# Attention over four heads at once, with the softmax sums on GpSimd and one VectorE reduce per two heads

## The reference, cut to what matters

```python
qkv = x @ w_qkv                                    # one sequence of 2048 rows, 16 heads of 32
q, k, v = jnp.split(qkv, 3, axis=-1)
q, k, v = (to_heads(q), to_heads(k), to_heads(v))
q = _rope(q, cos, sin)
k = _rope(k, cos, sin)
scores = jnp.einsum('bhqd,bhkd->bhqk', q, k) / jnp.sqrt(jnp.float32(HD))
scores = jnp.where(causal, scores, -jnp.inf)
attn = jax.nn.softmax(scores, axis=-1)
y = jnp.einsum('bhqk,bhkd->bhqd', attn, v)
```

## Time and profile before

| | |
|---|---|
| median of 3 runs | 2595.11 us (2592.67 to 2601.68) |
| the profiled execution's own time | 2602.47 us |
| its span, first to last instruction | 2600.7 us |
| attention stage, from its first DMA to the read of its result | 1050.4 to 1774.4 us |
| whole span: PE, DVE, ACT, POOL busy | 84%, 59%, 42%, 8% |

### The profile page before, as it was taken

The page is one execution under the profiler, slowest core; times in us unless marked ns, Lnnn a source line. Parts: engine busy times, 40 slices in busy tenths (PEclk is TensorE's granted clock), DMA queues, the critical chain, the costliest instruction groups (busy, mean ns, idle before and its releaser), DMA issues. The chain is left out here.

```text
span 2600.7 us, 43768 instructions
## 1 busy us (share of the span) xinstructions
PE 2190.7 (84%) x18800; PEld 1252.6 (48%) x18800; DVE 1537.1 (59%) x2400; ACT 1085.5 (42%) x1046; POOL 199.2 (8%) x225
## 2 busy tenths in 40 slices
PE   6799999999966997699999999993861399999990
PEld 3444444444433442344444444441360388888880
DVE  7768888888848099665665665541345244434423
ACT  5668888888814111044444444441110123223210
POOL 0000000000010043000000000001402200000005
PEclk9899999999988999599999999996955599999995
DMA  7311111121160223402220222006201523323307
GB/s 249 124 40 69 69 47 57 68 69 49 40 251 20 81 113 121 122 8 56 58 51 10 56 58 56 5 9 140 65 17 57 210 105 108 135 106 110 110 25 266
DMA packets 81360, 221.63 MB, mean 85 GB/s; under 512 B 10384, under 2 KB 11536, under 8 KB 72816
## 3 DMA queue, kind: packets, MB, share of 16 engines
q1 hardware_dynamic: 70080, 176.76, 21.2%
q0 software_dynamic: 11088, 42.08, 4.5%
HBM read 154.98 MB, written 59.51 MB: 82 GB/s over the span
## 5 line engine op out<-in xcount | busy, mean ns | idle before, releaser
L449 ACT ACTIVATE m_step<-m_ub,gat_bias 128x2048 bf16<-128x2048 f32 x256 | 494.0, 1992 | 120.6 <-DVE m_mask L526 109.5
L1057 DVE TENSOR_REDUCE t_rm<-t_m 128x1 f32<-128x512 f32 (+3 forms) x640 | 373.5, 608 | 238.7 <-PE t_m L1106 184.2
L1015 ACT ACTIVATE t_E<-t_s 128x1024 f32<-128x1024 f32 (+1 forms) x320 | 292.0, 938 | 424.2 <-PE t_s L1122 222.8
L526 DVE TENSOR_TENSOR m_mask<-m_step,gat_adjT 128x2048 bf16<-128x2048 bf16 x256 | 306.7, 1222 | 84.0 <-ACT m_step L449 72.1
L1106 PE MATMUL t_m<-t_K,t_Q 96*128 96x512 f32 (+3 forms) x640 | 262.3, 445 | 58.1 <-POOL t_trik L994 32.6
L1143 PE MATMUL t_o<-t_E,t_v 128*32 128x512 f32 (+1 forms) x1280 | 282.0, 560 | 0.0
L1143 PE MATMUL t_o<-t_E,t_ones 128*32 128x512 f32 (+1 forms) x1280 | 282.0, 560 | 0.0
L1106 PEld LDWEIGHTS t_m<-t_K,t_Q 96*128 96x128 f32 x640 | 117.3, 197 | 212.4 <-issue 89.5
L566 PE MATMUL m_bd<-m_mask,m_S 128*32 128x512 bf16 x3072 | 211.9, 380 | 8.0 <-DVE m_mask L526 7.7
L1122 PE MATMUL t_s<-t_Q,t_K 97*128 97x512 f32 (+1 forms) x640 | 216.2, 413 | 0.0
L566 PE MATMUL m_bd<-gat_adjT,m_S 128*32 128x512 bf16 x3072 | 211.5, 380 | 4.8 <-PE m_dn L566 4.8
(11 more groups left out here) (278 smaller groups left out, 3126.3 us busy)
## 6 DMA issues: line engine op xcount, KB each, us to landing
a_adj<-in_adj SPq DMA_DIRECT2D x16, 1024.0 KB, 4.9
m_ub<-scratch_uac SPq DMA_DIRECT2D x16, 1024.0 KB, 4.7
e_w1r<-in_L_ffn_w SPq DMA_DIRECT2D x8, 2048.0 KB, 8.0
e_w2r<-in_L_ffn_w SPq DMA_DIRECT2D x8, 2048.0 KB, 8.6
t_Q<-scratch_parts SPq DMA_DIRECT2D x42, 256.0 KB, 6.1
t_K<-scratch_parts SPq DMA_DIRECT2D x42, 256.0 KB, 8.2
scratch_xe<-o_zeros POOLq DMA_DIRECT2D x10, 1024.0 KB, 19.1
e_xe<-scratch_xe SPq DMA_DIRECT2D x8, 1280.0 KB, 9.1
```

The source lines that it names most:

```text
L449: act.activation(step[n % RELUS][:, :], ub[h % 2][:, :], ACT.Relu, bias=bias[:, j, h:h + 1], scale=BIG).then_inc(step_ready, 1)
L526: dve.tensor_tensor(mask[n % MASKS][:, :], step[n % RELUS][:, :], adjT[:, j, :], ALU.min).then_inc(mask_ready, 1)
L1015: act.activation(E[s % 2][hh][:, :, 0:w], ps_s[hh][:, :].rearrange("p (b n) -> p b n", b=2)[:, :, 0:w], ACT.Exp, scale=SCALE).then_inc(exp ...
L1057: dve.tensor_reduce(rm[:, hh, t, ch:ch + 1], ps_m[i % 2][:, 0:w], AX, ALU.max).then_inc(entry_read, 1)
```

## The change

Four heads (a quad) are worked on at once: four quads, 40 steps of one key tile each (160 in all), with queries cut at the diagonal to `BANK - off`. Scores of heads 0, 1 (z = 0) and 2, 3 (z = 1) lie in the four banks of `ps_s`; one exponential covers two heads. `E` has three buffers. TensorE's matmuls with ones no longer read `E`: GpSimd adds the exponentials of two steps into `total`, and `denominators` multiplies that by ones once in two steps, into a bank of its own (`ps_d`), which ScalarE copies out. `values` has four matmuls with the values of four heads, read from `V` (the copy into `v` goes). A piece of the maxima is made for two heads, in the two banks of the single `ps_m`, and one reduce reads both. A piece waits for the one right before it (`entry_read`, n, with nothing given in advance). A quad has 80 such pieces and 4 turns. 14 entries run ahead; the first quad has 70 more in its first 21 steps (`own_until`), and each quad makes 42 of the next one's in its last 19 (`next_until`). Q has one buffer, reloaded chunk by chunk. The rows of ones in K are set by GpSimd, and stores are issued apart for results and denominators.

```diff
-    for c in range(NC):
-        STEPS += [(c, kt, 0, BANK) for kt in range(0, 4 * c, 2)]
-        STEPS += [(c, 4 * c, 0, BANK), (c, 4 * c + 2, 2 * P, 2 * P)]
+    QUADS, G = H // 4, 4
+
+
+    STEPS = [(c, kt, max(0, kt - 4 * c) * P) for c in range(NC) for kt in range(4 * c + 4)]
     NS = len(STEPS)
...
     def pieces(c):
-        return [(hh, t, ch, BANK if ch < t // 4 else (t % 4 + 1) * P)
-                for hh in range(2) for t in range(4 * c, 4 * c + 4) for ch in range(c + 1)]
...
-            at += n + more
-    assert at == ahead, (at, ahead)
+    FIRST_OF = {c: min(i for i, (kind, p) in enumerate(ENTRIES) if kind == "piece" and p[1] // 4 == c) for c in range(NC)}
+
+
+    HALF = NS // 2
+    def even(s, s0, s1, n0, n1):
+        return n0 + (n1 - n0) * (s + 1 - s0) // (s1 - s0)
+
+    AHEAD = 8 + 1 + 16 + 1 + 16
+    def own_until(q, s):
+        if q == 0:
+            if s < 2:
+                return even(s, 0, 2, START, 25)
+            if s < 9:
+                return even(s, 2, 9, 25, 50)
+            return even(min(s, HALF), 9, HALF + 1, 50, NE)
+        return even(min(s, HALF), 0, HALF + 1, AHEAD, NE)
+
+    def next_until(q, s):
+        if q == QUADS - 1 or s <= HALF:
+            return 0
+        return even(s, HALF + 1, NS, 0, AHEAD)
+    START = 14
+
+
+    SUMS = [0]
+    for k in range(QUADS * NS // 2):
+        SUMS.append(SUMS[k] + (2 if STEPS[2 * k % NS][2] < STEPS[(2 * k + 1) % NS][2] else 1))
...
+        Q = st.sb("Q", [P, G, N], F32R)
+        K = [st.sb(f"K{r}", [P, G, N], F32R) for r in range(2)]
+        E = [st.sb(f"E{i}", [P, G, BANK]) for i in range(3)]
+        total = st.sb("total", [P, G, BANK])
...
-        ps_s = [st.ps(f"s{hh}", [P, 2 * BANK]) for hh in range(2)]
-        ps_o = [st.ps(f"o{i}", [P, BANK]) for i in range(2)]
-        ps_m = [st.ps(f"m{i}", [P, BANK]) for i in range(2)]
...
+        ps_s = st.ps("s", [P, G, BANK])
+        ps_o, ps_d = st.ps("o", [P, BANK]), st.ps("d", [P, BANK])
+        ps_m = st.ps("pm", [P, 2, BANK])
...
+                load_k(1)
+                for q in range(QUADS):
+                    more = q + 1 < QUADS
+                    if more:
+                        load_q(q + 1, 0)
+                    store(q, 0)
...
-                for j in range(H // 4):
-                    for r in range(2):
-                        pool.wait_ge(v_free[r], j + 1)
-                        col = (j * 4 + 2 * r) * DH
-                        pool.tensor_copy(v[r][:, :, :, :].rearrange("p t h d -> p t (h d)"),
-                                         V[:, :, ds(col, 2 * DH)]).then_inc(v_in[r], 1)
+                    pool.memset(K[r][ROWS:K1, :, :].bitcast(F32), 1.0).then_inc(k_ones[r], 1)
+                    pool.wait_ge(k_ones[r], 1)
+                for k in range(QUADS * NS // 2):
+                    a = 2 * k
+                    wide, off = STEPS[a % NS][2], STEPS[(a + 1) % NS][2]
+                    if k >= 1:
+                        pool.wait_ge(den_done, k)
+                    for z in range(2):
+                        pool.wait_ge(exp_done[z], a + 2)
+                        two = slice(2 * z, 2 * z + 2)
+                        if wide < off:
+                            pool.tensor_copy(total[:, two, wide:off], E[a % 3][:, two, wide:off]).then_inc(summed[z], 1)
+                        pool.tensor_tensor(total[:, two, off:BANK], E[a % 3][:, two, off:BANK],
+                                           E[(a + 1) % 3][:, two, off:BANK], ALU.add).then_inc(summed[z], 1)
...
+                if u >= 2:
+                    act.wait_ge(d_sent[u % 2], 64 * (u // 2))
+                act.activation(den[u % 2][:, :], ps_d[:, :], ACT.Copy).then_inc(d_copied, 1)
...
+                    for z in range(2):
+                        act.wait_ge(s_full[z], n + 1)
+                        if n >= 3:
+                            act.wait_ge(pv_done, n - 2)
+                            act.wait_ge(summed[z], SUMS[(n - 3) // 2 + 1])
+                        two = slice(2 * z, 2 * z + 2)
+                        act.activation(E[n % 3][:, two, off:BANK], ps_s[:, two, off:BANK], ACT.Exp,
+                                       scale=SCALE).then_inc(exp_done[z], 1)
+
+                    if n >= 3 and (n - 3) % NS in END.values():
+                        u = (n - 3) // NS * NC + STEPS[(n - 3) % NS][0]
+                        denominators_out(act, u)
+                denominators_out(act, QUADS * NC - 1)
...
-                    dve.tensor_reduce(rm[:, hh, t, ch:ch + 1], ps_m[i % 2][:, 0:w], AX, ALU.max).then_inc(entry_read, 1)
+                    h, t, ch, w = what
+                    dve.tensor_reduce(rm[:, h:h + 2, t, ch], ps_m[:, :, 0:w], AX, ALU.max).then_inc(entry_read, 1)
...
+                        pe.wait_ge(m_ready, q * NC + what + 1)
+                        if n >= 1:
+                            pe.wait_ge(entry_read, n)
...
+                    h, t, ch, w = what
...
+                    if n >= 1:
+                        pe.wait_ge(entry_read, n)
+                    diag = ch == c
+                    for z in range(2):
+                        mm = pe.matmul(ps_m[:, z, 0:w], Q[0:ROWS, h + z, t * P:(t + 1) * P],
+                                       K[q % 2][0:ROWS, h + z, ch * BANK:ch * BANK + w], start=True, stop=not diag)
                     if diag:
-                        mm = pe.matmul(ps_m[i % 2][:, w - P:w], ident_b[:, :], triq[:, :], start=False, stop=True)
+                        for z in range(2):
+                            mm = pe.matmul(ps_m[:, z, w - P:w], ident_b[:, :], triq[:, :], start=False, stop=True)
                     mm.then_inc(entry_full, 1)
...
+                    if n >= 1:
+                        pe.wait_ge(exp_done[z], n)
...
+                    for h in (2 * z, 2 * z + 1):
+                        mm = pe.matmul(ps_s[:, h, off:BANK], K[q % 2][0:K1, h, kt * P:(kt + 1) * P],
+                                       Q[0:K1, h, c * BANK + off:(c + 1) * BANK], start=True, stop=not diag)
...
+                    mm.then_inc(s_full[z], 1)
...
+                def values(n):
+                    q, s = divmod(n, NS)
+                    c, kt, off = STEPS[s]
+                    if kt == 0 and n:
+                        pe.wait_ge(o_copied, q * NC + c)
+                    for z in range(2):
+                        pe.wait_ge(exp_done[z], n + 1)
+                    for h in range(G):
+                        mm = pe.matmul(ps_o[h * DH:(h + 1) * DH, off:BANK], V[:, kt, (q * G + h) * DH:(q * G + h + 1) * DH],
+                                       E[n % 3][:, h, off:BANK], start=(kt == 0), stop=(kt == 4 * c + 3))
+                    mm.then_inc(pv_done, 1)
+
+                def denominators(k):
+                    q, s = divmod(2 * k, NS)
+                    c, kt, off = STEPS[s]
+                    last = kt == 4 * c + 2
+                    if kt == 0 and k:
+                        pe.wait_ge(d_copied, q * NC + c)
+                    for z in range(2):
+                        pe.wait_ge(summed[z], SUMS[k + 1])
+                    for h in range(G):
+                        mm = pe.matmul(ps_d[h * DH:(h + 1) * DH, off:BANK], ones[:, :], total[:, h, off:BANK],
+                                       start=(kt == 0), stop=last)
+                    mm.then_inc(den_done, 1)
+
+                pe.wait_ge(setup, 5)
+                own, coming = START, 0
+                for i in range(START):
+                    entry(0, i)
+                for z in range(2):
+                    scores(0, z)
+                for q in range(QUADS):
...
+                        n = q * NS + s
+                        upto, later = own_until(q, s), next_until(q, s)
+                        done = 0
+                        whole = upto - own + later - coming
...
+                            goal = ((whole + 1) // 2, (whole + 1) // 2, whole)[g]
+                            while own < upto and done < goal:
+                                entry(q, own)
                                 own += 1
...
+                                done += 1
+                            while coming < later and done < goal:
+                                entry(q + 1, coming)
+                                coming += 1
+                                done += 1
+                            if g < 2 and n + 1 < QUADS * NS:
+                                scores(n + 1, g)
+                        if n >= 2 and n % 2 == 0:
+                            denominators(n // 2 - 1)
+                        values(n)
+                    own, coming = coming, 0
+                denominators(QUADS * NS // 2 - 1)
```

More of the change, by code:

```diff
@@ L856, in pieces @@
     def pieces(c):
-        return [(hh, t, ch, BANK if ch < t // 4 else (t % 4 + 1) * P)
-                for hh in range(2) for t in range(4 * c, 4 * c + 4) for ch in range(c + 1)]
+        return [(h, t, ch, BANK if ch < t // 4 else (t % 4 + 1) * P)
```

(70 more changed lines are left out.)

309 lines of the change are left out of this document (90 added, 219 removed).

## The result

| | before | after |
|---|---|---|
| median of 4 runs | 2594.38 us (2592.67 to 2601.68) | 2668.69 us (2663.10 to 2673.70) |
| the profiled execution's own time | 2602.47 us | 2664.31 us |
| its span | 2600.7 us | 2662.1 us |
| first scores, last copy | 1094.0, 1770.2 us | 1087.0, 1831.1 us |
| read of the stage's result | 1774.4 us | 1837.4 us |

The change makes the kernel slower: ratio 1.028, 95% interval 1.0247 to 1.0313. Between the profiled executions the read of the stage's result moves by 63.0 us and the whole time by 61.8, so all of it is in this stage.

A forecast was written before the change was run, and what follows sets the result against it. TensorE's program order was taken to bound the kernel before; after, waits at the hand-over of pieces spend the saving. 2602.5 + 7 + 50 = 2659.5 us profiled, less 7.4 for the median: 2652 us, range 2598 to 2706.

The forecast's parts named there:

- The hand-over of a piece: Each two-head piece waits for the reduce of the one before: 2.04 us round trip, 2.51 with values and denominators.
- What leaves TensorE: TensorE's matmuls in the stage: 80 groups of values or ones fewer, 69 us; scores lose 7 us.
- The quads: Times of the stage's four quads: near 250, 170, 170 and 140 us.
- The clock: TensorE's clock in the stage: first 21 steps largely at 1.2 GHz, 38 us; later falls 12; together +50.
- ten falls: Drops of TensorE's clock behind the first 21 steps: ten at 1.2 us each, 12 us.
- Sums and the ends: GpSimd's adds of 1024 columns take 2.4 us; main part starts 5 us sooner; +3 us behind the last copy.
- the ring: Last 19 steps: two sums in the single `total`, then denominators, then the next sums, 6.1 us for two steps.
- GpSimd beside VectorE: VectorE's scaling of maxima could wait for a GpSimd sum, 16 times, up to 38 us; none was put in.
- the last one: Step from profiled execution to median: 7.4 us taken off 2659.5, giving 2652 us.
- the main part: Stage from first scores to last copy: 685 us expected at 2.4 GHz, 9 more than the 676 before.

The follow-up runs named there:

- The filling: The changed kernel with throwaway zero-weight matmuls between neighbouring pieces of the first quad and between the 14 entries ahead: 2644.75 us, ratio 1.0184.
- the kernel with the sums by heads: The changed kernel, but the one buffer of GpSimd's sums is handed over to and from TensorE by two heads: 2664.47 us, ratio 1.0258.

## Why the prediction was right

It said 2652 us (2598 to 2706), slower; the median is 2669. By its steps:

- **The hand-over of a piece.** Expected 2.04 us, with a reduce of 1.23; measured 2.05 and 1.226. With denominators 2.51 expected, 2.40 to 2.52 measured. The experiments confirm that this is the mechanism: a shorter reduce or a second buffer each give over 100 us.
- **What leaves TensorE.** The 69 us can't be read off one row. From the first piece to the last copy TensorE is busy for 684 of 713 us before and for 648 of 774 in after, and the 648 hold the stretches at half speed. The kernel with one-head pieces shows that some 42 us of them can be had.
- **The quads.** Expected 250, 170, 170 and 140; measured from the first scores and the copies:

```profile
1086.98 0.63 PE L1155 MATMUL t_s<-t_Q,t_K 97*128 97x512 f32 x1
...
1350.22 0.68 DVE L1065 COPY t_out<-t_o 128x512 f32<-128x512 f32 x1
...
1519.24 0.68 DVE L1065 COPY t_out<-t_o 128x512 f32<-128x512 f32 x1
...
1691.41 0.68 DVE L1065 COPY t_out<-t_o 128x512 f32<-128x512 f32 x1
...
1831.09 0.69 DVE L1065 COPY t_out<-t_o 128x512 f32<-128x512 f32 x1 [44.20 <-PE t_o L1169]
```

  263.2, 169.0, 172.2 and 139.7, in sum 744 us for the 735 of my sum (685, and 50 for the clock). The last three come to 480.9 us for 480; the 13 us over are all in the first. The next point's estimate of the clock's price there is what I took, so they should lie in what that quad costs at 2.4 GHz, and I can't say in which part.
- **The clock.** It fell as forecast. Ahead of the first scores 2.51 us pass from a full piece to the next one, and TensorE waits 1.3 us for the reduce:

```profile
1076.66 1.19 PE L1137 MATMUL t_pm<-t_K,t_Q 96*128 96x512 f32 x2 [1.41 <-DVE t_rm L1087]
1079.17 0.69 PE L1137 MATMUL t_pm<-t_K,t_Q 96*128 96x128 f32 x2 [1.32 <-DVE t_rm L1087]
```

  That is 0.47 over the trip at 2.4 GHz, where I had 0.4. For the first quad I took 38 us. The filling raised the mean clock of 1100 to 1260 us from 0.69 to 0.895 and gave 26 us; carried on to 1.00 in proportion, that is an estimate of 39. Behind the first quad I took ten falls; from its last copy to the last of all the clock is low seven times, 27 us together, and what they cost wasn't measured. The Trainium skill (TensorE: Matmul & The Clock Gate, Part 1) has half rate as what an idle engine falls back to, and under "A second HAM failure mode" (HAM is its name for the block that sets the clock) tells of a kernel in which TensorE idles briefly but often between groups of matmuls and its clock swings between the two levels. The trace agrees with the second: 0.63 and 0.75 in stretches where, by the timeline, no gap between matmuls was longer than 1.33 us (1087 to 1260 us).
- **Sums and the ends.** An add of 1024 took 2.37 us (2.4 expected), the ring 6.02 (6.1), and it bound the steps without pieces alone. First scores 7.0 us sooner (5 expected); from last copy to read 6.3 us for 4.1 (+2.2; +3 expected).
- **GpSimd beside VectorE.** Of VectorE's instructions in the stage it touched the scaling of the maxima, as suspected, and no other. One line of after, then the same line of before (min/median/max ns):

```profile
L1092 DVE TENSOR_SCALAR t_m<-t_m x16: 174/175/1561, 1076.8 to 1777.1; 128x16 f32<-128x16 f32 x16
```

```profile
L1062 DVE TENSOR_SCALAR t_m<-t_m x32: 170/171/173, 1066.2 to 1740.5; 128x8 f32<-128x8 f32 x32
```

  Three of the 16 took 1.56 us, at 1275.87, 1447.05 and 1617.05 us. Each began inside an add of GpSimd and ended with it; the other 13, at 0.17, ran beside no add. The trace names nobody who waited for `t_m`, and the two pieces in between do cover its turn, but the next reduce stands behind it on VectorE:

```profile
1275.04 4.66 POOL L1026 TENSOR_TENSOR t_total<-t_E 128x1024 f32<-128x1024 f32 x2 [4.17 <-PE t_d L1182]
...
1275.77 0.70 PE L1137 MATMUL t_pm<-t_K,t_Q 96*128 96x512 f32 x2
1275.87 1.56 DVE L1092 TENSOR_SCALAR t_m<-t_m 128x16 f32<-128x16 f32 x1
...
1277.58 1.23 DVE L1087 TENSOR_REDUCE t_rm<-t_pm 128x2 f32<-128x1024 f32 x1
1278.86 0.69 PE L1137 MATMUL t_pm<-t_K,t_Q 96*128 96x128 f32 x2 [2.39 <-DVE t_rm L1087]
```

  The round trip is 3.09 us (1275.77 to 1278.86) for 2.05, so this costs 1 us, three times. At two of the three places the clock fell too, 0.62 in 1278 to 1287 us and 0.72 in 1616 to 1628; at the one near 1447 it stayed at 1.00. I had put in nothing, because I looked for a wait in front of the turn and not in front of the next reduce; the term is small, some 3 us and what the two falls cost.

The term that was off is the last one: I took 7.4 us off, as if the changed kernel's profiled execution too stood above its median. It stood 4 us below, so that 2659.5 against 2664.3 for the profiled execution, a miss of 5 us, became 17 between the medians. The other misses are inside the main part (9 us).

## What to carry to other kernels

One instruction over two banks saves its engine little when the cost goes by columns (1.226 us for 2 x 0.689), but it turns two buffers into one: producer and consumer then take turns, and what is freed elsewhere is spent in that wait. Before merging two buffers, take one full trip, producer start to producer start, and lay the work between two pieces beside it. And when a change has several parts, build the ones that don't depend on each other alone: all that isn't the pieces, the sums on GpSimd among it, was worth 42 us, hidden here under a loss of 118.

## What was not expected of the hardware

In the later quads TensorE's clock differs between the kernels without following the work that TensorE has. The doubled scores (busy for 73 of 80 us where after has 69) had 0.91 in two stretches, and behind the filled first quad three stretches fell to 0.91, where after had 0.94 to 0.98. But the kernel with the sums by heads has after's matmuls and no more, and it fell to 0.94 and 0.87 where after had 1.00 and 0.98; so these falls can't be put down to the added work. In after, falls begin at two of the three held scalings above, around the change to the last quad (1691.6 and 1701.8 us) and elsewhere; what makes such a place lose the clock in one kernel and hold it in the next stays open. It goes along with the spread of after's runs: the two at 2663 and 2664 us had a mean clock of 0.894 and 0.892 over the whole program, the two at 2673 and 2674 had 0.889. No experiment here was made for it. The other surprise is that throwaway matmuls can make a kernel faster, 24 us here, and that they stop doing so once the waits that they fill are gone.
